# Row gathers of the first layer in two lots of four, each lot behind a landing instead of behind TensorE's transposes

## The reference, cut to what matters

```
h = relu(edge_attr @ W1 + b1)                       # 412500 x 256
w_edge = (h @ W2 + b2).reshape(-1, 16, 16)
msgs = einsum('ei,eio->eo', x[src], w_edge)         # x[src]: one row of 16 for each edge
aggr = segment_sum(msgs, dst, num_segments=n_nodes)
```

## Time and profile before

| | |
|---|---|
| median of 3 runs | 8238.7 us (8236.46 to 8240.17) |
| span of the profiled execution | 8221.3 us |
| its own time around the span | no separate figure is given; the median of the runs is 17.4 us above the span |
| first gather to last gather of the first layer | 62.0 to 4962.4 us |
| PE, DVE, POOL busy share of the span | 89%, 81%, 69% |
| granted TensorE clock, 200 to 4900 us and 5200 to 8100 us | 0.92 and 1.00 |

### The profile page before, as it was taken

The page is one execution under the profiler, slowest core; times in us unless marked ns, Lnnn a source line. Parts: engine busy times, 40 slices in busy tenths (PEclk is TensorE's granted clock), DMA queues, the critical chain, the costliest instruction groups (busy, mean ns, idle before and its releaser), DMA issues. The chain is left out here.

```text
span 8221.3 us, 191064 instructions
## 1 busy us (share of the span) xinstructions
PE 7349.2 (89%) x52997; PEld 6446.6 (78%) x52997; DVE 6691.0 (81%) x17449; ACT 4457.4 (54%) x8279; POOL 5696.0 (69%) x4866
## 2 busy tenths in 40 slices
PE   7888888888888888888888886999999999999998
PEld 5667676666676666666676765999999999999996
DVE  6777777777777777777777777999999999999997
ACT  3333333333333333333333335888888878778884
POOL 6666666666666666666666664888888888888886
PEclk8999999999999999999999998999999999999999
DMA  2000000000000000000000014444444455554443
GB/s 60 18 17 17 17 17 17 17 17 17 17 17 17 17 18 17 17 17 18 17 17 17 17 23 101 73 75 74 74 75 74 74 73 74 72 74 75 73 75 64
DMA packets 713464, 341.73 MB, mean 42 GB/s; under 512 B 422115, under 2 KB 656599, under 8 KB 713427
## 3 DMA queue, kind: packets, MB, share of 16 engines
q1 hardware_dynamic: 379313, 272.94, 13.1%
q0 software_dynamic: 332928, 64.86, 12.9%
q10 hardware_dynamic: 1186, 3.51, 0.1%
HBM read 307.85 MB, written 32.96 MB: 41 GB/s over the span
## 5 line engine op out<-in xcount | busy, mean ns | idle before, releaser
L802 POOL DMA_INDIRECT xg<-gather_rows,idx x3132 | 3041.9, 971 | 1882.4 <-issue 1848.5
L919 PE MATMUL ps_w<-W2s,hT 128*128 128x256 f32 x12928 | 3240.2, 408 | 37.1 <-issue 36.6
L919 PEld LDWEIGHTS ps_w<-W2s,hT 128*128 128x128 f32 x12928 | 2678.5, 207 | 581.6 <-issue 97.0
L1745 POOL DMA_INDIRECT sums<-total,row x1616 | 2551.0, 1579 | 529.1 <-issue 474.4
L1708 PE MATMUL ps_wide<-hot_col,placed 128*128 128x392 f32 x12928 | 2434.7, 345 | 4.8 <-DVE placed L1544 2.1
L1708 PEld LDWEIGHTS ps_wide<-hot_col,placed 128*128 128x128 f32 x12928 | 2313.6, 196 | 12.2 <-issue 6.9
L841 ACT ACTIVATE hT<-ps_h,b1c 128x512 f32<-128x512 f32 x1616 | 1022.8, 680 | 2302.1 <-PE ps_h L905 2090.8
L1002 DVE TENSOR_TENSOR prod<-ps_w,xg 128x512 f32<-128x512 f32 x1616 | 1098.1, 690 | 969.7 <-remote 599.7
L1544 DVE SCALAR_TENSOR_TENSOR placed<-ps_r,src_r,halves 128x512 fp32r<-128x512 f32 x1616 | 1097.5, 741 | 0.1
L1643 ACT ACTIVATE square<-iota_col,minus_col 128x784 bf16<-128x784 int16 x1212 | 1061.3, 938 | 66.6 <-issue 58.0
L1009 DVE TENSOR_REDUCE msg<-prod 128x32 f32<-128x512 f32 x1616 | 1058.9, 676 | 0.0
(11 more groups left out here) (229 smaller groups left out, 5425.0 us busy)
## 6 DMA issues: line engine op xcount, KB each, us to landing
dst_row<-dst_rows SPq DMA_DIRECT2D x404, 256.0 KB
src_row<-src_rows SPq DMA_DIRECT2D x404, 128.0 KB
xg<-gather_rows,idx POOLq DMA_INDIRECT x3132
q_win<-q_rows SPq DMA_DIRECT2D x404, 96.0 KB
ea<-in_edge_attr SPq DMA_DIRECT2D x404, 64.0 KB
sums<-total,row POOLq DMA_INDIRECT x1616
e<-in_edge_attr SPq DMA_DIRECT2D x404, 32.0 KB
q_rows<-Q SPq DMA_DIRECT2D x12, 768.0 KB, 5.4
```

What stands on the lines that cost most here:

```text
L802: pool.indirect_dma_start(xg[r][:, t, :], None, k.rows, bass.IndirectOffsetOnAxis(ap=idx[r][:, t:t + 1], axis=0)).then_inc(xg_in[r][t], 16)
L919: last = pe.matmul(to, hT[half][:, j, col:col + P], k.W2[:, j, :], start=(j == 0), stop=(j == 1 and not with_b2))
L1745: pool.indirect_dma_start(k.sums[t], bass.IndirectOffsetOnAxis(ap=row[r][:, t:t + 1], axis=0), total[r][:, t, :], None, compute_op=ALU.add ...
```

## The change

The gathers of a group are issued in two lots: tiles 0 to 3, and tiles 4 to 7 (4 to 6 where seven are gathered). Ahead of its first gather each lot waits for the landing of the last but one gather of the lot in front: the second lot for tile 2 of its own group, the first lot for tile 6 (5) of the group before. The wait for `e_turned` is gone. `idx_ready` and `msg_ready` stay, and `gathers_begun` is counted up once a lot.

```
 def gather(g, r, use):
     pool.wait_ge(q["idx_ready"], g + 1)
     need(pool, q["msg_ready"], g - RING + 1)
-    if not (isinstance(g, int) and g < 2):
-        pool.wait_ge(q["e_turned"], g + 1)
+    if not (isinstance(g, int) and g == 0):
+        r0, use0 = (r - 1) % RING, use - (r == 0)
+        pool.wait_ge(xg_in[r0][gathered(r0, use0) - 2], 16 * (use0 + 1))
     pool.sem_inc(q["gathers_begun"], 1)
-    for t in range(T - 1 if dense(r, use) else T):
+    for t in range(gathered(r, use)):
+        if t == 4:
+            pool.wait_ge(xg_in[r][t - 2], 16 * (use + 1))
+            pool.sem_inc(q["gathers_begun"], 1)
         pool.indirect_dma_start(
```

More of the change, by code:

```diff
@@ L794, in _, with gathered @@
             def _(pool):
+                def gathered(r, use):
+                    return T - 1 if dense(r, use) else T
                 def gather(g, r, use):
```

## The result

The changed kernel takes 9145.59 us (median of 4 runs, 9141.74 to 9151.72) against 8239.44 us of the kernel before on the same chip (8236.46 to 8240.65): ratio 1.1102, 95% interval 1.1086 to 1.1118. It is 906 us slower. 7904 was forecast.

A forecast was written before the change was run, and what follows sets the result against it. The first layer was taken as bound by a gather-made core stall closed through `e_turned`: 12.13 us a group falls to 11.3 (10.9 floor plus 0.4), times 404 is 335 us off the median, 7904 us; range 7540 to 8420.

The forecast's parts named there:

- What bounds the kernel: First layer: no engine full; a whole-core stall from gathers issued too fast, closed into a round by `e_turned`, 12.13 us a group.
- 1.4 us a gather: First layer: rate at which something digests gathers, read from groups of seven and eight; POOL issues them every 1.25 us.
- the prediction's floor: First layer: digestion at 1.4 us for each of 7.75 gathers allows no less than 10.9 us a group.
- the gain of 0.83 us a group: First layer: forecast fall of the group period from 12.13 to 11.3 us, 335 us over 404 groups.
- Lots of four at 5.5 us are 1.37 us a gather: POOL's gathers: lots run nearly at the digestion rate of 1.4 us, so the stall should become short or vanish.
- This gate closes only when POOL is a full group ahead: POOL's wait for `idx_ready`: indices are made a group further ahead than gathers need; argument against the slower outcome.
- the lots come at a bad moment: The slower rival: POOL stands behind ACT's indices, 14.7 us a group, 1050 us more, 9289 us; chance 0.24.
- the gate 2.6 us later in the round: POOL's lot behind `idx_ready` would start at 2516.2 instead of 2513.62, adding 2.6 us to the 12.13 us group.
- L and W: POOL's landing waits: L, gather start to landing, 2.2 us; W, from there to the next gather's start, 0.8 us.
- POOL's floor: First layer: least group time by POOL's lots and landing waits, 10.7 us, from 10.3 to 11.2.
- The first rival: First layer: the pause only moves, digestion goes on as before, 12.16 us a group, 8251 us; chance 0.16.
- PE's clock: First layer: mean granted clock 0.92, expected to rise a little if PE idles less; nothing counted for it.

The follow-up runs named there:

- The paces: Kernel before with an extra POOL instruction behind a group's gathers, widening the step from 1.25 to between 1.31 and 1.68 us; ratios 0.9922 to 1.0351.
- the best kernel that was run: Kernel before with a 32-column POOL multiplication behind every gather (two behind the last of seven), `e_turned` kept; 8173.75 us, ratio 0.9922.
- the one with 8 columns of pace: Kernel before with an 8-column POOL multiplication behind each of a group's first seven gathers, `e_turned` kept; step 1.46 us, ratio 1.0047.

## Why the prediction was wrong

*What bounds the kernel: right.* A round closed through a stall of the whole core, which comes from gathers issued too close. The paces show that much: at 1.68 us a gather no wait for "remote" is left. What it is that the gathers exhaust stays open.

*1.4 us a gather: the size was off.* Stalls stop holding POOL between 1.46 and 1.52 us, and short ones are left at 1.55. At 1.52, 7.75 gathers are 11.8 us a group, where the prediction's floor had 10.9. That alone takes away most of the gain of 0.83 us a group: the best kernel that was run measured 12.05 us a group and not 11.3.

*"Lots of four at 5.5 us are 1.37 us a gather, nearly its rate, so the backlog hardly grows and the stall should become short or vanish": this step failed.* The lots came at 5.66 us, 1.41 a gather, and the stall ended 11.69 us behind the group's first gather where it had ended at 11.52. A lot's 0.65 us of gap is too little against what is left over from each gather, and the run with lots and `e_turned` shows the same by its time, 1.0017. The stall's length goes with the number of gathers, 11.52 and 11.69 us for eight and 10.11 for seven. That it does not go with the moment of the last one shows in that run and in the one with 8 columns of pace, whose last gather is issued some 1.4 us later for 0.5% more time.

*"This gate closes only when POOL is a full group ahead": the step that turned the sign.* It was the argument against the slower rival, and it is true, but being a full group ahead is what removing `e_turned` does. `e_turned` at g + 1 admitted POOL to group g in PE's body g - 2. The indices of group g are made in ACT's body g - 3, one body earlier: so without the wait POOL moves up one group, once, and from then on stands at `idx_ready` (360 times in 404 groups). The counts of the three gates were in the text of the kernel, and one line of bookkeeping would have said so.

*The rival "the lots come at a bad moment" was right in its mechanism and nearly in its price.* It said 14.7 us for all groups and 9289 us. Measured: 14.84 us in the group shown, 14.41 in the mean, as a group of seven is shorter here too, 9146 us. Its term, the gate 2.6 us later in the round, measured 2.2 us (3.15 from the release to the gather, against 0.94), and the stall itself ended 0.17 us later. Lots had no part in it: the removal alone cost 1.1159. Its chance of 0.24 was too low, since the only reason against it did not hold.

*L and W: right.* 3.16 us for 3.0. (The low end of POOL's floor is 10.4 us by the prediction's own terms and not 10.3; nothing in the forecast hangs on it.) The Trainium skill's fixed cost of about 2.0 us ("DMA: Bandwidth & Descriptors", section "Anatomy of one DMA"), counted behind the descriptors, would have made it 3.74 by estimate. But that section lists descriptor generation among the parts of its 2.0 us, and counted from the gather's start the trace comes near to it: 3.16 less the 0.8 to 0.9 of W is about 2.3 us.

*The first rival, the pause only moves,* is what the lots do by themselves (1.0017). The second layer was untouched, as said. PE's clock was left out of the sum; it fell by 0.04, as PE idled more.

## What to carry to other kernels

Before a wait is removed, write down for each of the waits that stay in which turn of the loop it opens, and by which engine's queue: the next one to close may stand behind a longer chain of the same stall. Here the gate that was removed stood 0.9 us behind the release and the next one 3.1, and with neither, POOL stood at a third, 9% slower with lots and 15% without. And where a stall comes from the rate of something, as here, starting the parts earlier gives nothing back, and lots did so only where neither gate held POOL: change the rate or the number, and try the rate first with an idle instruction behind each.

## What the runs showed of the hardware

Indirect gathers of 128 rows of 128 bytes, issued by POOL every 1.25 us, hold up the whole core: hidden-layer matmuls that stand among PE's rows at 2511.16 let ACT go only at 2517.52. At 1.51 us behind seven gathers of eight ACT had 308 waits for "remote" in 4700 us, at 1.52 behind every gather 94, at 1.55 42, at 1.68 none. In the groups shown the stall ends 11.52 and 11.69 us behind the first of eight gathers and 10.11 us behind the first of seven, about 1.45 us a gather. What is exhausted, the descriptors' ring, the notification of landings or something else, no run here shows; nor was it tried whether other sizes of gather have the same rate.

A fill of 0.20 us on POOL behind a gather lengthens the step by only 0.06 us, as the idle time ahead of the next gather falls from 0.30 to 0.17 us. A multiplication of 0.26 us (8 columns) lengthens it by 0.21: with it the gather itself takes longer too (1.01 us for 0.95).
